# Graph layer 2: one feature-by-node sum feeds both layer norms, and GpSimd works out the edge weight's term

## The reference

```python
x_l = (x @ W_l + b_l).reshape(n, H, C);  x_r = (x @ W_r + b_r).reshape(n, H, C)
e_emb = (ea @ W_e).reshape(-1, H, C)          # ea: one weight per edge, the mean for loops
x_j = x_l[src]
m = leaky_relu(x_j + x_r[tgt] + e_emb, 0.2)
logits = einsum('ehc,hc->eh', m, att)
...                                           # softmax per target, sum of alpha * x_j
out = gelu(out + bias, approximate=False)
h = out + x
layer2 = (h - mu) * rsqrt(var + 1e-5) * ln_w + ln_b
x = _layernorm(x + layer2)                    # the outer norm
```

## Time and profile before

| | us |
|---|---|
| median of three runs | 3526.74 |
| lowest, highest | 3514.69, 3531.47 |
| profiled execution, its own time | 3540.14 |
| its span, first to last instruction | 3538.4 |
| PE, DVE busy | 2701.9 (76%), 2616.7 (74%) |
| ACT, POOL busy | 2012.3 (57%), 1863.6 (53%) |

### The profile page before, as it was taken

How to read it: one execution, slowest core, us unless ns; L and a number is a source line. 1 busy time by engine, 2 the same in 40 slices (tenths; PEclk the granted TensorE clock), 3 DMA queues, 4 the chain that set the end, 5 groups by cost and what they waited for, 6 DMA issues and landing times. The chain is left out here.

```text
span 3538.4 us, 46258 instructions
## 1 busy us (share of the span) xinstructions
PE 2701.9 (76%) x14325; PEld 1792.3 (51%) x14325; DVE 2616.7 (74%) x3171; ACT 2012.3 (57%) x3400; POOL 1863.6 (53%) x1771
## 2 busy tenths in 40 slices
PE   7799999689999778878785789999999774332332
PEld 3466666466666545555553246666666553221221
DVE  6589999889999868888884269999999994222322
ACT  0167777556665558878784258888888782111111
POOL 4477787333333276766663654554453003666665
PEclk6699999899999989999997899999999996566655
DMA  6357666556666556666662156666666653222221
GB/s 202 100 173 222 212 221 220 189 176 197 197 202 199 160 167 207 210 207 208 197 205 74 47 159 172 188 196 193 183 194 174 183 171 107 58 64 63 74 69 39
DMA packets 474800, 573.34 MB, mean 162 GB/s; under 512 B 65347, under 2 KB 283133, under 8 KB 474431
## 3 DMA queue, kind: packets, MB, share of 16 engines
q1 hardware_dynamic: 412744, 457.19, 42.0%
q0 software_dynamic: 56480, 111.88, 11.6%
q10 hardware_dynamic: 5334, 1.32, 0.2%
HBM read 353.51 MB, written 220.55 MB: 162 GB/s over the span
## 5 line engine op out<-in xcount | busy, mean ns | idle before, releaser
L1292 POOL DMA_INDIRECT g_xd_xs<-table_x,dst_row x196 | 211.8, 1081 | 360.4 <-PE g_psT L1358 250.7
L1804 POOL DMA_INDIRECT f_xs<-table_x,src_row x196 | 192.0, 980 | 312.5 <-POOLq L1216 253.1
L775 POOL DMA_INDIRECT c_xs<-table_x,src_row x196 | 185.5, 946 | 303.9 <-PE c_psT L916 250.6
L765 POOL DMA_INDIRECT c_xs<-table_h,src_row x196 | 206.9, 1056 | 193.0 <-PE c_psT L909 94.0
L1867 ACT ACTIVATE f_reluT<-f_psY 128x512 f32<-128x512 f32 x49 | 29.3, 597 | 472.6 <-DMA table_x<-g_x3o 329.2
L497 POOL DMA_INDIRECT xs<-in_x,src_i x196 | 224.7, 1147 | 101.6 <-issue 54.0
L482 POOL DMA_INDIRECT xd<-in_x,dst_i x196 | 222.9, 1137 | 96.3 <-issue 47.9
L1811 POOL DMA_INDIRECT out<-f_xo,end_i x196 | 198.7, 1014 | 121.1 <-DVE f_xo L1904 61.6
L1292 POOL DMA_INDIRECT g_xd_xs<-table_x,src_row x196 | 218.6, 1116 | 59.8 <-issue 59.8
L765 POOL DMA_INDIRECT c_xd<-table_h,dst_row x196 | 200.8, 1025 | 59.8 <-issue 59.8
L1363 PE MATMUL g_psP<-w_center,g_turns 128*128 128x128 f32 x1568 | 197.1, 279 | 13.6 <-ACT g_turns L1492 9.1
(11 more groups left out here) (330 smaller groups left out, 8669.8 us busy)
## 6 DMA issues: line engine op xcount, KB each, us to landing
g_share<-shares SPq DMA_DIRECT2D x196, 192.0 KB
xn<-in_x SPq DMA_DIRECT2D x49, 512.0 KB
table_x<-xo SPq DMA_DIRECT2D x49, 512.0 KB
table_x1b<-xb SPq DMA_DIRECT2D x49, 512.0 KB
c_xn<-table_x SPq DMA_DIRECT2D x49, 512.0 KB
table_h<-c_xo SPq DMA_DIRECT2D x49, 512.0 KB
c_xn<-table_h SPq DMA_DIRECT2D x49, 512.0 KB
c_x1r<-table_x1b SPq DMA_DIRECT2D x49, 512.0 KB
```

Of the source, the lines that this page charges most:

```text
L765: pool.indirect_dma_start(out=quarters(rows[:, s, :])[j], out_offset=None, in_=table, in_offset=edge_index(columns, now.n, j)).then_inc(la ...
L775: pool.indirect_dma_start(out=quarters(xs[:, s, :])[j], out_offset=None, in_=table, in_offset=edge_index(h.src_row, now.n, j)).then_inc(sr ...
L1292: pool.indirect_dma_start(out=quarters(xd_xs[:, s, k, :])[j], out_offset=None, in_=table, in_offset=edge_index(columns, now.n, j)).then_in ...
L1804: pool.indirect_dma_start(out=quarters(xs[:, s, :])[j], out_offset=None, in_=table, in_offset=edge_index(h.src_row, now.n, j)).then_inc(sr ...
```

## The change

What it does:

- In set-up, PE and DVE make two matrices: `twice_centred` = center times diag(ln_w) times center, and `ln_b_row`, the centred ln_b in every partition.
- `gx` = gelu result plus x, both feature by node (a new DVE addition; for the edge rows x is first turned into `psU`). The centring product of `gx` is squared straight from PSUM for `var1`; it is no longer kept. A second product of the same `gx`, with `twice_centred`, is scaled by `rstd1` straight from PSUM into `pre2`. `pre1`, `n1`, its turning back and `affT` are gone.
- x and ln_b are added as rows: POOL adds `ln_b_row` to the loaded rows (three blocks of 512, in place), and DVE adds the result to `pre2`.
- `sq1` and `sq2` have a buffer each. `sq2` is taken an iteration later, directly behind the gelu on ACT. `var2` stands behind the `gx` additions on DVE.
- The edge weights are loaded into all 128 partitions (a broadcast DMA of 2 KB to 256 KB). POOL multiplies them by w_e, adds b_r, and then adds the `values` of the tile. PE's product with `w_e_row` is gone, and DVE's `z` adds POOL's term to `psZ`.

```diff
+            def add_weights(n):
+                pool.wait_ge(erow_landed[n % 2], 16 * (n // 2 + 1))
+                nc.gpsimd.tensor_scalar(erow[:, n % 2, :], erow[:, n % 2, :], h.col("w_e"), h.col("b_r"), ALU.mult,
+                                        ALU.add).then_inc(factored, 1)
+                pool.wait_ge(factored, n + 1)
+                pool.wait_ge(v_kept, n + 1)
+                nc.gpsimd.tensor_tensor(erow[:, n % 2, :], erow[:, n % 2, :], values[:, n % ring, 0, :],
+                                        ALU.add).then_inc(term_ready, 1)
+            for n in range(ends):
+                if is_tile(n):
+                    gather(n)
+                if is_tile(n - 1):
+                    add_weights(n - 1)
+                e = n - 2 - lag
+                if is_tile(e):
+                    pool.wait_ge(n_turned, e + 1)
+                    pool.wait_ge(xe_turned, e + 1)
+                    x = by_row(rows[:, e % 4, :, :].rearrange("p b n -> p (b n)"))
+                    nc.gpsimd.tensor_tensor(x, x, bias, ALU.add).then_inc(biased, 1)
...
-                wait(sp, z_ready, n - 1)
-                sp.dma_start(erow[0:1, n % 2, :], io["ew1"][:, n * TILE:(n + 1) * TILE]).then_inc(erow_landed[n % 2], 16)
+                wait(sp, z_added, n - 1)
+                sp.dma_start(erow[:, n % 2, :], io["ew1"][:, n * TILE:(n + 1) * TILE]
+                             .to_broadcast([P, TILE])).then_inc(erow_landed[n % 2], 16)
...   (TensorE)
                 if is_tile(e1):
-                    pe.wait_ge(gn_ready, e1 + 1)
+                    pe.wait_ge(x2e_landed[e1 % 4], 16 * (e1 // 4 + 1))
+                    wait(pe, scaled_e, e1 - 1)
+                    turned_rows(psU[:, 0, :], rows[:, e1 % 4, 2, :]).then_inc(xe_turned, 1)
+                    pe.wait_ge(gxn_ready, e1 + 1)
                     for k in range(2):
-                        ins = centred(psP[:, k, :], gn[:, k, :])
+                        ins = to_rows(psP[:, k, :], gx[:, e1 % 2, k, :], h.w["center"])
...
-                if is_tile(e2):
-                    pe.wait_ge(n1_ready, e2 + 1)
-                    pe.wait_ge(n_kept, min(e0 + 1, STEPS))
-                    for k in range(2):
-                        ins = turned_rows(psT[:, k, :], n1[:, k, :])
-                    ins.then_inc(n1n_turned, 1)
-                    pe.wait_ge(pre1e_ready, min(e1 + 1, STEPS))
-                    turned_rows(psU[:, 0, :], n1[:, 2, :]).then_inc(n1e_turned, 1)
...
-                    nc.tensor.matmul(psZ[:, 0, :], h.w_e_row[:, :], erow[:, c % 2, :],
-                                     start=False, stop=True).then_inc(z_ready, 1)
...
                 if is_tile(e2):
-                    pe.wait_ge(affn_ready, e2 + 1)
-                    pe.wait_ge(pre1n_ready, min(e1 + 1, STEPS))
+                    pe.wait_ge(sq1n_ready, min(e1 + 1, STEPS))
+                    wait(pe, scaled_n, e2)
                     for k in range(2):
-                        ins = centred(psP[:, k, :], affT[:, k, :])
+                        ins = to_rows(psP[:, k, :], gx[:, e2 % 2, k, :], h.twice_centred)
...   (ScalarE: affT, the old sq1 and the old place of sq2 go)
+                if is_tile(e3):
+                    act.wait_ge(pre2_ready, e3 + 1)
+                    wait(act, var2_ready, e3)
+                    nc.scalar.activation(sq2[:, :, :], pre2[:, :, :], ACT.Square).then_inc(sq2_ready, 1)
...
+                    nc.scalar.activation(sq1[:, 0:2, :], psP[:, :, :], ACT.Square).then_inc(sq1n_ready, 1)
+                    act.wait_ge(ee_ready, e1 + 1)
+                    nc.scalar.activation(sq1[:, 2, :], psU[:, 0, :], ACT.Square).then_inc(sq1e_ready, 1)
...   (VectorE: n1, pre1 and the two additions of pre2 go)
+                if is_tile(e1):
+                    dve.wait_ge(gn_ready, e1 + 1)
+                    dve.wait_ge(n_kept, e1 + 1)
+                    nc.vector.tensor_tensor(gx[:, e1 % 2, 0:2, :], gx[:, e1 % 2, 0:2, :], nodeT[:, e1 % 2, :, :],
+                                            ALU.add).then_inc(gxn_ready, 1)
+                    dve.wait_ge(ge_ready, e1 + 1)
+                    dve.wait_ge(xe_turned, e1 + 1)
+                    nc.vector.tensor_tensor(gx[:, e1 % 2, 2, :], gx[:, e1 % 2, 2, :], psU[:, 0, :],
+                                            ALU.add).then_inc(gxe_ready, 1)
...
+                    scaled(pre2[:, 0:2, :], psP[:, :, :], rstd1[:, e2 % 2, 0:8], 2, scaled_n)
                 if now:
                     dve.wait_ge(z_ready, c + 1)
-                    dve.wait_ge(v_kept, c + 1)
+                    dve.wait_ge(term_ready, c + 1)
                     wait(dve, zl_ready, c)
-                    nc.vector.tensor_tensor(z[:, :], psZ[:, 0, :], values[:, c % ring, 0, :],
+                    nc.vector.tensor_tensor(z[:, :], psZ[:, 0, :], erow[:, c % 2, :],
                                             ALU.add).then_inc(z_added, 1)
...
+                    scaled(pre2[:, 2:3, :], psU[:, :, :], rstd1[:, e2 % 2, 8:12], 1, scaled_e)
+                    dve.wait_ge(biased, e2 + 1)
+                    dve.wait_ge(scaled_n, e2 + 1)
+                    dve.wait_ge(scaled_e, e2 + 1)
+                    nc.vector.tensor_tensor(pre2[:, :, :], pre2[:, :, :], rows[:, e2 % 4, :, :],
+                                            ALU.add).then_inc(pre2_ready, 1)
```

More of the change, by code:

```diff
@@ L1237, in layer2 @@
         agg = sb("agg", [P, 2, TILE])
-        pre1, n1, pre2, sq, turns, x3o = (sb(n, [P, 3, TILE]) for n in ("pre1", "n1", "pre2", "sq", "turns", "x3o"))
-        sq1, sq2 = sq, sq
-        gn, ge, affT = turns[:, 0:2, :], turns[:, 2, :], turns
+        gx = sb("gx", [P, 2, 3, TILE])
+        pre2, sq1, sq2, x3o = (sb(n, [P, 3, TILE]) for n in ("pre2", "sq1", "sq2", "x3o"))
         x4o = sb("x4o", [P, 2, TILE])
-        var1, lnv1, rstd1 = (sb(n, [P, 12]) for n in ("var1", "lnv1", "rstd1"))
+        var1, lnv1, rstd1 = sb("var1", [P, 12]), sb("lnv1", [P, 12]), sb("rstd1", [P, 2, 12])
         var2, lnv2, rstd2 = sb("var2", [P, 12]), sb("lnv2", [P, 20]), sb("rstd2", [P, 20])
@@ L1283, in _, with gather @@
         def _(pool):
-            def step(t):
-                now = t.tile(0)
-                s = now.slot
-                wait(pool, src_landed[s], 64 * now.half)
-                wait(pool, dst_landed[s], 64 * now.half)
-                wait(pool, e_turned, now.n - 1)
+            def gather(n):
+                s = n % 2
+                wait(pool, src_landed[s], 64 * (n // 2))
+                wait(pool, dst_landed[s], 64 * (n // 2))
+                wait(pool, e_turned, n - 1)
                 for k, columns, landed in ((0, h.dst_row, dst_landed), (1, h.src_row, src_landed)):
@@ L1463, in _ @@
                     wait(pe, n_kept, e0 + 1)
-                    wait(pe, affn_ready, e2 + 1)
                     turn_edges(c + 1)
@@ L1491, in _ @@
                     wait(act, fn_ready, e1 - 1)
-                    nc.scalar.activation(gn[:, :, :], psP[:, :, :], ACT.Gelu, bias=h.bl_out[:, :],
+                    nc.scalar.activation(gx[:, e1 % 2, 0:2, :], psP[:, :, :], ACT.Gelu, bias=h.bl_out[:, :],
                                          scale=1.0 / (1.0 + DEN_EPS)).then_inc(gn_ready, 1)
@@ L1500, in _ @@
                     wait(act, y_ready, e0 - 1)
+                    wait(act, gxn_ready, e0 - 1)
                     nc.scalar.activation(nodeT[:, e0 % 2, :, :], psT[:, :, :], ACT.Copy).then_inc(n_kept, 1)
@@ L1562, in _ @@
                     act.wait_ge(lnv1_ready, e1 + 1)
-                    wait(act, n1_ready, e1)
-                    nc.scalar.activation(rstd1[:, :], lnv1[:, :], ACT.Exp, scale=-0.5).then_inc(rstd1_ready, 1)
-                if is_tile(e2):
-                    act.wait_ge(pre2n_ready, e2 + 1)
-                    act.wait_ge(pre2e_ready, e2 + 1)
-                    act.wait_ge(var1_ready, min(e2 + 2, STEPS))
-                    nc.scalar.activation(sq2[:, :, :], pre2[:, :, :], ACT.Square).then_inc(sq2_ready, 1)
+                    wait(act, scaled_e, e1 - 1)
+                    nc.scalar.activation(rstd1[:, e1 % 2, :], lnv1[:, :], ACT.Exp, scale=-0.5).then_inc(rstd1_ready, 1)
         @block.vector
@@ L1681, in _ @@
                 e0, e1, e2, e3 = (c - k - lag for k in range(4))
-                if is_tile(e2):
-                    dve.wait_ge(rstd1_ready, e2 + 1)
-                    wait(dve, n1n_turned, e2)
-                    wait(dve, n1e_turned, e2)
-                    scaled(n1[:, :, :], pre1[:, :, :], rstd1[:, :], 3, n1_ready)
+                if is_tile(e0):
+                    v = values[:, e0 % ring, :, :]
+                    dve.wait_ge(share_landed[e0 % 2], 64 * (e0 // 2 + 1))
+                    nc.vector.tensor_tensor(v, v, share[:, e0 % 2, 1:3, :], ALU.mult).then_inc(weighed, 1)
+                    dve.wait_ge(weighed, e0 + 1)
+                    nc.vector.tensor_tensor(v[:, 0, :], v[:, 0, :], v[:, 1, :], ALU.add).then_inc(summed, 1)
+                if is_tile(e1):
```

(7 more changed lines are left out.)

130 lines of the change are left out of this document (51 added, 79 removed).

## The result

The changed kernel takes 3705.3 us (median of 4 runs, 3694.4 to 3715.4), the kernel before beside it 3526.6 (3514.7 to 3531.5). The ratio is 1.050, its 95% interval 1.047 to 1.053. Slower was forecast, but 179 us is three times the 58 of the forecast and lies outside its range. The direction was right and the size was not.

What follows compares the result with a forecast made beforehand. It took a loop through DVE, ACT and PE, with DVE having least room, to set the iteration. Long stage +44, first +6 and last +8, together +58 on 3526.7, gave 3585 us; range 3500 to 3645.

Steps and rivals of the forecast that it cites:

- DVE's own work is equal, the 0.78 us wait for `sq1` goes, and part of a stall can hide in the wait before `x3o`: Layer 2's iteration: DVE work 5.555 against 5.557 us, loop becomes 16.78, about 0.6 us of stall hidden.
- POOL's three operations at 4.6 us, ends 2.6 and 6.6: POOL, each iteration: the scaling of 512 and additions of 512 and 1536 take 4.6 us, between 2.6 and 6.6.
- DVE loses 0.55 x 4.6 = 2.5 us, less 0.6: Long stage, each iteration: POOL holds DVE's two-SBUF-operand work, a share of 0.55, for 2.5 us; 1.9 stay.
- The long stage: Layer 2 from 2100 to 2728 us, 34 iterations: 34 x 1.9 - 21.2 = +44 us.
- Rival D: POOL mostly gives way to DVE, which loses about 0.6 us net an iteration: 3525 us, no change; chance 0.20.
- PE's saving becomes idle time: PE: removed transposes and product, some 2.4 us an iteration end to end, shorten no part of the loop; priced at nothing.
- PE falls by 60 to 80 us: Sign on PE: it falls by 60 to 80 us and the iteration doesn't follow.
- First stage +6: Layer 2's first stage: gathers also wait for `values` and the addition behind it; +6 us, +30 at most.
- Last stage +8: Layer 2's last stage: only the bias addition, 1.5 us ten times, less 6.6 us; +8.
- Rival B: POOL becomes the bound, needing 19.0 us an iteration, and DVE loses 3.6: 3644 us; chance 0.13.
- What would show A: Signs of the forecast (3585 us, chance 0.47): DVE's two-SBUF-input operations longer or late, near 65 us over 34 iterations.

Runs made afterwards that it cites:

- e3: The changed kernel with the edge weight's product on TensorE as before and the addition of ln_b left out; 3504.2 us (ratio 0.994).
- e13: e2 with POOL's addition of ln_b also waiting for DVE's scan, so that it starts with `x3o`; 3727.8 us (ratio 1.058).
- e2: The changed kernel with the edge weight's product back on TensorE and the value addition back on VectorE; GpSimd keeps the ln_b addition; 3560.4 us (ratio 1.009).
- e17: The changed kernel with TensorE making the last product of a tile's norms three times over; ratio 1.039.
- e18: e13 with TensorE making the last product of a tile's norms three times over; ratio 1.037.
- e12: The changed kernel with TensorE turning rows 16 times more into a free `psT` before it waits for `psP`; 3709.5 us (ratio 1.054).
- e7: The changed kernel with the addition of ln_b issued as twelve additions of 128 columns in place of one of 1536; 3683.0 us (ratio 1.045).
- e4: The changed kernel with the addition of ln_b replaced by three writes of zeros over the same 1536 columns; 3572.4 us (ratio 1.015).
- e14: The change's norms part alone, with the ln_b addition between destination and source gathers, started after `x4o`; 3533.4 us (ratio 1.001).
- e15: The whole change with the addition of ln_b placed as in e14; 3624.7 us (ratio 1.029).
- e16: e14 with the addition of ln_b as three additions of 512 columns; ratio 1.002.

## Why the prediction was wrong in size

- *DVE's own work is equal, the 0.78 us wait for `sq1` goes, and part of a stall can hide in the wait before `x3o`*: right. e3, which has only this, has a tile of 16.55 us (16.78 forecast), and in the ordinary tiles of the changed kernel both waits of DVE in the earlier trace rows are gone or covered.
- *POOL's three operations at 4.6 us, ends 2.6 and 6.6*: 4.6 was too low, though the measured time lies inside the ends. Alone they take 0.77, 1.27 and 3.42, together 5.5, and 6.4 as they run beside DVE. The forecast took a middle where rows bore on neither end. The estimate with the figure of the Trainium skill (GPSIMD Engine Reference, section 3.1) was 5.2; the trace has 5.5, so the page's figure was the better one.
- *DVE loses 0.55 x 4.6 = 2.5 us, less 0.6*: this is the step that failed. The factor 0.55 is the chance that a POOL operation meets one of DVE's with two inputs, if it can fall anywhere. But its place is fixed. The end of `values` starts POOL's addition of 512, and the scan and `x3o` start 0.6 and 2.4 us behind it. DVE loses 3.5 us in an ordinary tile, and up to 3.2 more in a tile with a maximum. e13 against e2 shows it: 167 us for a shift of 3.7 us. The long stage came out at +141.6 us and not at +44. Rival D's "POOL gives way" was partly true, for who starts first holds the other until its instruction ends.
- *PE's saving becomes idle time*, priced at nothing: this is the second step that failed. It holds for the work removed (e3's PE is busy 48 us less). But the idle time that the stall added is not free. The granted clock fell, and 1.57 us a tile came on top, through a wait that the forecast had missed altogether: DVE's L1704 now waits for the turned edge rows. e17 prices it at 41 us of the 179, of which its trace places 32 in the long stage. In e18, where POOL's queue isn't the next limit, it is 75, with 40 in the long stage. *PE falls by 60 to 80 us* came out as 0.7.
- *First stage +6*: -4. POOL is late for `z` there (104 us of waits by DVE), but DVE waited 93 us for `z` there before, and the stage as a whole got no longer.
- *Last stage +8*: +26.8. In its last seven tiles an operation of 0.69 us is held 3.2 us, because the addition starts just ahead of it each time. That makes 22 us.
- *Rival B*, 3644, came nearest in time, but not by its mechanism: POOL still waited 93.8 us for `values` in the long stage, over some 28 tiles. Its queue came up as the next limit only when the clock was kept (e12, e17: an ordinary tile takes 19.66 us with no wait of POOL).
- *What would show A*: the lines named were the right ones and carry the excess. They were forecast at 65 us in the long stage. Over the layer `x3o`, the scan and the values' sum alone carry 117.
- The Trainium skill (SBUF — State Buffer, Who interferes with whom) has it that the later of the two blocks fully, for the whole instruction, and that a GpSimd instruction that only writes is no party to it. The traces agree in both directions, 0.69 to 3.87 us for DVE and 3.42 to 4.36 for POOL. e7 agrees with the length and e4 with the exception. The forecast cited the rule and then weakened it to an average.
- Not settled: the 9.2 us in layers that the change doesn't touch, which lie within the spread of runs of one kernel (17 us in before); and where the part of e17's and e18's gain lies that their long stages don't show.

## What to carry to other kernels

When two engines hold each other, don't multiply a duration by a share of busy time. Lay both timelines over each other at the semaphore that starts the second engine, and read which instruction is due next: here a shift of 3.7 us was worth 167. Put GpSimd's long reading operation beside instructions of VectorE that have at most one input in SBUF. Then look at the tiles where the order differs, for there it may meet another victim (e14, e15 and e16 each had one). Last, look at what a stall does to the clock of the engine that waits for it.

## What the runs showed of the hardware that was not expected

- More work on TensorE made a kernel faster: two repeated products of 1.06 us a tile took the ratio from 1.058 to 1.037. The product behind a 3.49 us pause took 3.64 us (granted clock 0.57 from 2362 to 2366 us of e13), and it takes 1.96 behind a pause of 1.37.
- GpSimd's addition of 1536 columns takes 3.42 us, of 512 columns 1.27, of 128 columns about 0.78 each (twelve in 9.37, with DVE at work). In twelve pieces it costs more than twice as much, part of which is turns given to DVE.
- VectorE's tiniest operations lose as much as its largest: 128x112 went from 0.27 to 3.42 us, 128x1536 from 1.76 to 4.79.
